# The scan's last step reads the gated sums from their PSUM bank

## The reference

```python
dA = jnp.exp(dt[..., None] * A)
dBx = dt[..., None] * B_ssm[:, :, None, :] * x_conv[..., None]
_, h = jax.lax.associative_scan(comb, (dA, dBx), axis=1)
y = jnp.einsum('btdn,btn->btd', h, C_ssm)
y = y * silu(z) + D_param * x_conv
out = jnp.einsum('btd,ed->bte', y, W_out)
```

## Time and profile before

| | |
|---|---|
| time, median of 3 runs | 2795.99 us |
| lowest and highest | 2795.15 and 2811.24 us |
| profiled execution | 2800.82 us |
| its span, first to last instruction | 2798.9 us |
| mean granted TensorE clock | 0.945 |

### The profile page before, as it was taken

The page is one execution under the profiler, slowest core; times in us unless marked ns, Lnnn a source line. Parts: engine busy times, 40 slices in busy tenths (PEclk is TensorE's granted clock), DMA queues, the critical chain, the costliest instruction groups (busy, mean ns, idle before and its releaser), DMA issues. The chain is left out here.

```text
span 2798.9 us, 37099 instructions
## 1 busy us (share of the span) xinstructions
PE 2359.9 (84%) x9792; PEld 1213.6 (43%) x9792; DVE 1940.0 (69%) x3181; ACT 1631.4 (58%) x4156; POOL 1736.1 (62%) x2247
## 2 busy tenths in 40 slices
PE   5889998989898999989889898989899998958433
PEld 3555544444444444444444444444444444422100
DVE  3444567686777768686776768686786868666776
ACT  3655566666666666666666666666666665533332
POOL 1012257585867858585866758586785857587543
PEclk9999999999999999999999999999999999978665
DMA  7424374665546565565546456555656465333442
GB/s 137 48 43 77 58 141 96 122 121 128 117 98 126 110 138 103 118 122 128 112 91 133 99 121 123 121 117 108 123 102 144 104 121 114 107 91 91 113 122 68
DMA packets 497981, 304.96 MB, mean 109 GB/s; under 512 B 349818, under 2 KB 416298, under 8 KB 497322
## 3 DMA queue, kind: packets, MB, share of 16 engines
q1 hardware_dynamic: 497772, 302.59, 52.9%
HBM read 242.21 MB, written 26.74 MB: 96 GB/s over the span
## 5 line engine op out<-in xcount | busy, mean ns | idle before, releaser
L1128 POOL TENSOR_TENSOR work<-work,bc 128x512 f32<-128x512 f32 x512 | 650.3, 1278 | 104.9 <-PE bank L1164 82.4
L1134 DVE TENSOR_TENSOR_SCAN work<-bank,work 128x512 f32<-128x512 f32 x512 | 621.2, 1213 | 109.3 <-POOL work L1128 83.5
L873 POOL TENSOR_TENSOR zh<-zh,w_bc 128x512 f32<-128x512 f32 x256 | 326.8, 1277 | 581.9 <-DVE zh L866 579.5
L1141 POOL TENSOR_TENSOR work<-work,bc 128x512 f32<-128x512 f32 x448 | 581.2, 1303 | 74.9 <-DVE work L1134 74.9
L1117 ACT ACTIVATE bank<-work,neg_a 128x510 f32<-128x510 f32 x512 | 351.5, 687 | 460.8 <-DVE work L1134 448.5
L532 PE MATMUL bank<-ke,q_all 96*128 96x256 f32 x2048 | 555.2, 395 | 12.0 <-DMA q_all<-q_rows 12.0
L549 ACT ACTIVATE probs<-bank,nmax 128x256 f32<-128x256 f32 x1024 | 473.6, 470 | 134.0 <-DVE nmax L539 131.9
L539 DVE TENSOR_REDUCE nmax<-bank 128x2 f32<-128x512 f32 x512 | 348.7, 681 | 233.0 <-PE bank L532 221.9
L532 PEld LDWEIGHTS bank<-ke,q_all 96*128 96x128 f32 x2048 | 382.1, 197 | 214.1 <-issue 163.2
L860 PE MATMUL bank<-h_b,w_t 128*128 128x512 f32 x512 | 297.4, 664 | 118.0 <-DVE zh L851 102.2
L559 PEld LDWEIGHTS bank<-ident,probs 128*128 128x128 f32 x2048 | 255.5, 144 | 242.6 <-issue 168.1
(11 more groups left out here) (192 smaller groups left out, 2528.4 us busy)
## 6 DMA issues: line engine op xcount, KB each, us to landing
work<-dt_rows SPq DMA_DIRECT2D x256, 512.0 KB, 5.3
w_bc<-w_rows_d SPq DMA_DIRECT2D x256, 256.0 KB, 4.4
ke<-ke SPq DMA_DIRECT2D x128, 256.0 KB, 5.0
bc<-bc_rows SPq DMA_DIRECT2D x64, 256.0 KB, 6.6
x_in<-in_x SPq DMA_DIRECT2D x32, 256.0 KB, 5.0
q_all<-q_rows SPq DMA_DIRECT2D x512, 8.0 KB
dt_rows<-step SPq DMA_DIRECT2D x16, 512.0 KB, 3.7
dt_rows<-step SPq DMA_DIRECT2D x32, 256.0 KB, 2.4
```

What stands on the lines that cost most here:

```text
L873: nc.gpsimd.tensor_tensor(zh[:, n % 3, :], zh[:, n % 3, :], w_bc[:, n % WB, :], ALU.mult).then_inc(m_p, 1)
L1128: nc.gpsimd.tensor_tensor(hb[at % HB], ring[n % RING][:, 1, :], bc[:, s, :], ALU.mult).then_inc(s_dbx, 1)
L1134: nc.vector.tensor_tensor_scan(hb[at % HB], decay_bank(p, m)[:, :], hb[at % HB], 0.0, ALU.mult, ALU.add).then_inc(s_h, 1)
L1141: nc.gpsimd.tensor_tensor(hb[at % HB], hb[at % HB], bc[:, SG + batch(m)[2], :], ALU.mult).then_inc(s_hc, 1)
```

## The change

Line 1171 writes its product back to bank 7, where it read the sums, instead of to `z_gate`. Line 1173 reads the product from bank 7 and writes `z_gate` as before. Since bank 7 is now in use until line 1173 has ended, the sums of the next half wait for `s_yv` instead of `s_g`. The order of instructions on every engine stays; there are as many as before.

```diff
@@ -1151,9 +1151,9 @@
         def s_sum_tensor(pe, p, m):
 
             if m == 3 and p:
-                pe.wait_ge(s_g, 2 * p)
+                pe.wait_ge(s_yv, 2 * p)
             if m == BATCHES // 2 + 3:
-                pe.wait_ge(s_g, 2 * p + 1)
+                pe.wait_ge(s_yv, 2 * p + 1)
@@ -1168,9 +1168,9 @@
         def s_end_vector(dve, p, h):
             dve.wait_ge(s_zg, 2 * p + h + 1)
             dve.wait_ge(s_y, BATCHES // 4 * p + BATCHES // 8 * (h + 1))
-            nc.vector.scalar_tensor_tensor(z_gate[:, h, :], z_gate[:, h, :], 0.5, bank[7][:, :], ALU.mult, ALU.mult).then_inc(s_g, 1)
+            nc.vector.scalar_tensor_tensor(bank[7][:, :], z_gate[:, h, :], 0.5, bank[7][:, :], ALU.mult, ALU.mult).then_inc(s_g, 1)
             dve.wait_ge(s_g, 2 * p + h + 1)
-            nc.vector.scalar_tensor_tensor(z_gate[:, h, :], x_conv(p, h), d_par[:, h:h + 1], z_gate[:, h, :],
+            nc.vector.scalar_tensor_tensor(z_gate[:, h, :], x_conv(p, h), d_par[:, h:h + 1], bank[7][:, :],
                                            ALU.mult, ALU.add).then_inc(s_yv, 1)
```

## The result

The change makes the kernel slower: median 2816.2 us (2803.4 to 2829.4, 17 runs) against 2797.8 (2785.2 to 2815.0, 17 runs), ratio 1.0078, 95% interval 1.0059 to 1.0097, so it is 0.8% slower, well clear of the noise. (Ratios here are the recorded ones, with their intervals; the plain quotient of the medians, 1.0066 here, can differ from them by up to 0.3% and lies inside the interval in every run.) The forecast was 2777 with a range of 2765 to 2795. The profiled execution took 2816.2 us, its span 2813.4.

What follows compares the result with a forecast made beforehand. No engine is full; VectorE's line 1173, waiting for GpSimd multiplies, delays TensorE. Savings of 17.0 for stalls, 5.1 for ordinary waits, 1.3 and smaller ones, together 24.3, take the profiled 2800.8 to 2776.5, forecast 2777 us, range 2765 to 2795.

Steps and rivals of the forecast that it cites:

- Line 1173 at 0.75 us everywhere: VectorE's line 1173, reading its product from PSUM, takes line 866's median of 0.75 us with no wait for GpSimd.
- Ordinary blocks 0.39 us shorter: In all 13 blocks line 1173's ordinary wait goes, 1.14 - 0.75 = 0.39 us each, 5.1 us together.
- The stalls of line 1173 gone: Three disturbed blocks, with line 1173 held up by GpSimd multiplies, fall back to ordinary length, saving 17.0 us.
- Writing PSUM costs nothing: Line 1171 writing over its PSUM input: nothing taken, with bounds of +0.01 us each and 0.38 us each, or 12 us.
- PSUM input no dearer: VectorE reading PSUM costs no more than SBUF: 680 ns for line 1171 against 692 for line 970.
- The estimate worked out from the fixed parts: 58 cycles for an SBUF source, 120 for PSUM: 0.065 us for each of 32 VectorE instructions, 2 us lost, 2779.
- The bank given back later costs nothing: TensorE's next sums wait for line 1173 instead of line 1171; 3.9 us of slack cover it, cost nothing.
- Line 607 is the next thing late, at 1.64 us: Behind line 1173, VectorE's line 607, also with two SBUF inputs, waits for GpSimd and takes 1.64 us.
- line 607 over 2 us: Sign that the forecast is wrong: a VectorE line 607 this long would mean the stall moved on.
- Rival 4: Line 607 inherits the stall: 3.7 us a block, 48 us in all 13, 2825; decides from about seven blocks; chance 0.06.
- None of its 64 executions takes over 1.75 us: Line 607's record in the profile before the change, cited against its inheriting a stall.
- Rival 1: Line 607 gains too, running at once if over 0.14 us earlier against GpSimd: 0.69 us, 12 us more, 2765; chance 0.12.

Runs made afterwards that it cites:

- e1: Changed kernel with the second attention group's line 607 left out from the second pair on; 2771.4 us, ratio 0.9907 to the kernel before.
- e6: Changed kernel with the second group's reciprocals in idle bank 3, so line 607 reads one PSUM and one SBUF tensor; 2769.7 us, ratio 0.9899.
- e12: Changed kernel plus a 64-column VectorE instruction with two SBUF inputs behind the first half's line 1173; 2807.1 us, ratio 1.0051.
- e2: Kernel before the change with the second group's line 607 left out from the second pair on; 2800.3 us, ratio 1.001.
- e7: Kernel before the change with the second group's reciprocals in bank 3 instead of SBUF for line 607; 2795.0 us, ratio 0.9996.
- e4: Changed kernel with the second group's lines 603 and 607 six steps later, step 40 instead of 34; 2809.1 us, ratio 1.0038.

## Why the prediction was wrong

- *Line 1173 at 0.75 us everywhere*: right, 0.746 to 0.749. *Ordinary blocks 0.39 us shorter*: 157.3 to 156.7, slightly more. *The stalls of line 1173 gone*: right, 17 us in the account above.
- *Writing PSUM costs nothing*: 0.010 us on the median of line 1171, 0.3 us in all. That is the cheap end of the prediction's bounds; the two ScalarE rows behind it differ in where they read as well as in where they write, so the agreement is partly luck. *PSUM input no dearer*: right. The estimate worked out from the fixed parts in the Trainium skill, "VectorE: DVE Perf Modes", section "The TRN2 errata", 0.065 us an instruction more, does not show in this trace: line 1173 has 746 ns as its shortest against 751 with SBUF.
- *The bank given back later costs nothing*: e1 and e6 leave no room for a cost there.
- *Line 607 is the next thing late, at 1.64 us*: this step failed. It was named as the next in line and its wait taken as fixed, so that the sum has no term for it. The runs showed it at 4.0 us in ten of 12 blocks, 4.2 us a block or 42 us in all, more than the 24.3 saved. The prediction's own sign for this, line 607 over 2 us, is what came. Rival 4, which describes it, got 0.06. That rival's size was right: 2.5 us more in the instruction (4.00 against 1.55) and 3.7 forecast against 4.2 measured for the block; it struck in ten blocks where seven decide. 2777 + 10 x 4.2 = 2819, the median is 2816.
- The evidence against rival 4 was misread. "None of its 64 executions takes over 1.75 us" was a row about line 607 behind a contested line 1173. The change took that contest away, and with it the shield (or the earlier place, which goes with it). In e12 a contested instruction of 64 columns in the same place brings the old handovers back. A record under one condition was used for the other.
- Rival 1 did not come: where line 607 is not passed over it still waits, 1.55 us against 1.64. VectorE came 0.39 us earlier, but GpSimd about 0.46, the time the contest had cost its multiply, so line 607 asks later in the same multiply, at 0.26 instead of 0.19 us (the prediction's 0.14 took the multiply to begin at 613.00; it begins at 612.95).
- The chances also took the stall as three unlucky blocks. That it was a lottery could be read from the spread of the runs (2795 to 2811), and I used it for the size of the gain only.

What stays open: why the first contested instruction is passed over seldom at line 1173's place (3 of 11 blocks in the kernel before, 3 of 12 in e2, 0 of 12 in e7), but in 8 to 11 of 11 or 12 at line 607's place when it is the first, and in ten of ten at e4's. The form is excluded, and so is the place within the multiply from 0.26 to 0.86 us; whether the shield is the contest itself or the shift of the two engines that it brings is not, and what a handover that VectorE wins leaves behind in GpSimd's queue no row shows.

## What to carry to other kernels

List the VectorE instructions with two SBUF inputs that run beside a row of GpSimd multiplies, and treat them as one group: freeing one can move the stall to the next, so change them together or count on nothing. One small operand in PSUM is enough to take an instruction out of the contest. An unhindered record of the next instruction is worth something only if the instruction ahead of it stays as it is, and a kernel whose runs spread by 1% while the ordinary blocks of its profile repeat to 0.2 us may have such a lottery somewhere.

## What was not expected of the hardware

- A VectorE instruction with two SBUF inputs can be passed over at every boundary of a row of GpSimd multiplies, and gets in only when GpSimd pauses: 4.82 us for an instruction of 0.75. In the profiles of the kernels before and after, none that was passed over once got in at a later boundary without a pause; the nearest to an exception is the one at 926.50 in the kernel before, which asks just as a multiply starts, waits for that one and gets in behind it (1.81 us).
- The pause may be as short as GpSimd's 0.09 us write without an input; 98 of them make the kernel before 0.49% faster.
- Without the contest the spread can nearly go: e6's six runs lie within 4.6 us, the 17 of the kernel before within 30. It is not the only source, as e1, with both instructions out of the contest, spreads over 15.
